# GpSimd's first root moved between its scatters, and its fifth scatter put behind the next group's first scores

## The reference

```python
x = x + conv_ref(_ln_c(x), W_qkv, b_qkv, W_proj, b_proj)   # windowed attention
t = _to_tokens(x)
t = t + ffn_ref(_ln_t(t), router_w, w1, w2, w3)            # mixture of experts
...
def _ln_c(v, eps=1e-06):
    m = jnp.mean(v, axis=-1, keepdims=True)
    s = jnp.var(v, axis=-1, keepdims=True)
    return (v - m) / jnp.sqrt(s + eps)
```

## Time and profile before

| what | us |
|---|---|
| median of 3 runs | 703.29 |
| range of the runs | 696.98 to 704.82 |
| the profiled execution's own time | 693.54 |
| its span, first to last instruction | 691.2 |
| PE busy | 593.7 (86%) |
| DVE busy | 484.2 (70%) |
| GpSimd busy | 440.0 (64%) |
| ACT busy | 414.2 (60%) |

### The profile page before, as it was taken

How to read it: one execution, slowest core, us unless ns; L and a number is a source line. 1 busy time by engine, 2 the same in 40 slices (tenths; PEclk the granted TensorE clock), 3 DMA queues, 4 the chain that set the end, 5 groups by cost and what they waited for, 6 DMA issues and landing times.

```text
span 691.2 us, 20144 instructions
## 1 busy us (share of the span) xinstructions
PE 593.7 (86%) x5359; PEld 368.5 (53%) x5359; DVE 484.2 (70%) x1692; ACT 414.2 (60%) x934; POOL 440.0 (64%) x398
## 2 busy tenths in 40 slices
PE   1888888888888888852889999999999999999991
PEld 0466566656665556542445555555555555555550
DVE  2578878888878767763556667777676777776772
ACT  1678777778767767641345556555565565565560
POOL 1111777767767766546557876775766868666776
PEclk9999999999999999965599999999999999999996
DMA  9900000100000000001143444444434434344342
GB/s 328 295 10 9 26 27 25 33 25 25 25 24 25 24 23 24 26 25 37 45 85 39 53 43 44 50 41 48 50 38 50 44 43 52 38 50 48 38 52 16
DMA packets 85590, 34.67 MB, mean 50 GB/s; under 512 B 81966, under 2 KB 82478, under 8 KB 85038
## 3 DMA queue, kind: packets, MB, share of 16 engines
q0 software_dynamic: 26640, 9.90, 15.0%
q1 hardware_dynamic: 58910, 24.30, 14.3%
HBM read 20.21 MB, written 13.76 MB: 49 GB/s over the span
## 4 chain that ended last, share of the span: by engine, by line
PE 51%; issue 7%; DMA 5%; POOL 5%; DVE 4%; POOLq 1%; ACT 1%; DVEq 0%; ACTq 0%
PE bank L504 21%; PE bank L518 13%; POOL expert_rows L1225 3%; PE bank L473 3%; DMA expert_rows<-rows,slot_u 3%; PE bank L451 2%; PE bank L509 2%; PE bank L441 2%; PE bank L463 2%; PE bank L634 2%; DMA out<-y_early,meta 1%; PE bank L528 1%; DMA out<-y_out,token 1%; DVE smax L960 1%; PE bank L435 1%
## 5 line engine op out<-in xcount | busy, mean ns | idle before, releaser
L1313 POOL DMA_INDIRECT out<-y_out,token x144 | 222.8, 1547 | 89.2 <-DVE y_out L1136 53.1
L1225 POOL DMA_INDIRECT expert_rows<-rows,slot_u x144 | 147.8, 1027 | 79.2 <-issue 27.5
L504 PE MATMUL bank<-xs,w_sb 64*128 64x384 f32 x510 | 182.2, 500 | 4.7 <-DVE hid L1175 1.8
L505 PE MATMUL bank<-xs,w_sb 64*128 64x384 f32 x510 | 182.5, 501 | 0.0
L779 ACT ACTIVATE gate_h<-bank 128x384 f32<-128x384 f32 x255 | 125.2, 492 | 61.2 <-PE bank L505 43.6
L1175 DVE TENSOR_TENSOR hid<-gate_h,bank 128x384 f32<-128x384 f32 x255 | 140.4, 554 | 30.2 <-ACT gate_h L779 13.2
L504 PEld LDWEIGHTS bank<-xs,w_sb 64*128 64x128 f32 x510 | 92.0, 189 | 88.2 <-issue 39.4
L518 PE MATMUL bank<-hid,w_sb 128*64 128x384 f32 x612 | 110.5, 496 | 2.7 <-DVE hid L1175 2.7
L505 PEld LDWEIGHTS bank<-xs,w_sb 64*128 64x128 f32 x510 | 92.0, 189 | 0.0
L789 ACT ACTIVATE y_odd<-bank 64x384 f32<-64x384 f32 x51 | 24.9, 487 | 85.9 <-PE bank L518 82.0
L1168 DVE TENSOR_TENSOR y_t<-y_odd,bank 64x384 f32<-64x384 f32 x51 | 27.8, 546 | 56.3 <-ACT y_odd L789 53.4
(11 more groups left out here) (136 smaller groups left out, 977.2 us busy)
## 6 DMA issues: line engine op xcount, KB each, us to landing
xin<-expert_rows SPq DMA_DIRECT2D x51, 99.0 KB
xin<-expert_rows SPq DMA_DIRECT2D x51, 96.0 KB
w_sb<-w SPq DMA_DIRECT2D x1, 3072.0 KB, 22.1
out<-res_all SPq DMA_DIRECT2D x18, 128.0 KB
expert_rows<-rows,slot_u POOLq DMA_INDIRECT x144
out<-y_out,token POOLq DMA_INDIRECT x144
x_all<-x_win SPq DMA_DIRECT2D x1, 1664.0 KB, 8.6
res_all<-x_res SPq DMA_DIRECT2D x1, 1664.0 KB, 12.1
```

Source lines behind the costliest of these rows:

```text
L504: pe.matmul(ps_h[c % RING], w13_sb[0:C, e, c, :], xs[0:C, :], start=True, stop=True)
L505: pe.matmul(ps_g[c % RING], w13_sb[C:2 * C, e, c, :], xs[C:2 * C, :], start=True, stop=True).then_inc(s_h, 1)
L1225: pool.indirect_dma_start(rows_dram, bass.IndirectOffsetOnAxis(ap=slot_u[:, spar, i // 2, i % 2:i % 2 + 1], axis=0), rows[:, spar, i // 2, ...
L1313: pool.indirect_dma_start(out, bass.IndirectOffsetOnAxis(ap=token[:, c:c + 1], axis=0), y_out[:, c, :], None, compute_op=ALU.add).then_inc ...
```

## The change

Only GpSimd's program is edited. Root 1 comes directly behind scatter 1. Scatters 2 and 3 follow it back to back, and the wait in front of scatter 2 is gone. The wait in front of scatter 4 is a new one: `scored(b)` waits until PE has finished the first scores of the next group (`s_score` reaches b + 1, which is the first score instruction of the next pass) instead of until DVE has subtracted in the fourth tile of this group.

```diff
+            def scored(tg):
+
+                after(pool, s_score, tg, 0)
+                hold(pool)
+
...
                 elif ok(send):
                     fill_meta(send, par)
                     scatter(par, (0, 1), par)
-                    softened(att_g, 2)
-                    scatter(par, (2,), par)
                 if ok(new):
                     root(ln1_rstd, ln1_vare, s1vare, s1rstd, s1xn, new)
                 if ok(send) and not drain:
-                    scatter(par, (3,), par)
-                    softened(att_g, 3)
+                    scatter(par, (2, 3), par)
+                    scored(b)
                     scatter(par, (4, 5), par)
```

## The result

In alternating runs on one chip the changed kernel took 704.45 us (median of 20 runs, 700.37 to 708.11) and the kernel before 700.0 us (20 runs, 695.93 to 705.45). The ratio is 1.0049, with a 95% interval of 1.0027 to 1.007: the change costs 1.9 to 4.9 us, and the forecast was a gain of 1.6. The time lies inside the range; the sign is wrong.

A forecast was written before the change was run, and what follows sets the result against it. The prediction took a circle of waits between DVE and PE as the bound, GpSimd outside it but disturbing L830. Terms of -1.4 and -0.2 us made -1.6, from 703.29 to 701.7 us, range 695.5 to 707.

The forecast's parts named there:

- The gain of 1.4 us from L830: DVE's L830, no longer beside scatter 2, takes 0.17 us less in 8 passes where PE waits for q: 1.4 us.
- 0.17 us less, with the q rotation behind it: In DVE's list, L830 falls from 0.34 us by 0.17 us, and q starts that much sooner.
- the 0.2 us: DVE's L858 takes 0.17 us, 0.03 less in 8 unmasked passes, before the next softmax: 0.2 us gained.
- covers: Slack before readers need GpSimd's later results; thinnest at L821 behind the centring, 0.77 us against 0.45 late in unmasked passes.
- the late centring: Rival, chance 0.09: DVE's L821 waits for GpSimd's centring in every pass; net 4.4 us slower, 707.7 us.
- Nothing comes of it: Rival, chance 0.12: PE's gap before L634 is largely its own issue, so earlier q buys little: 703.3 us.
- The disturbance only moves: Rival, chance 0.10: scatter 4 starts sooner and holds L858 as L830 was; 1.1 us come back, 703.0 us.
- L858 sits out scatter 4: Rival, chance 0.08: DVE's L858 is held until scatter 4 ends, 0.47 us more in 8 unmasked passes: 705.7 us.
- Within 1%: Whole kernel's time within about 1% (7 us) of the kernel before, chance 0.83; faster 0.09, slower 0.08.
- the spread of the runs: Rival, chance 0.15, on the whole time: three runs of one kernel lie 7.8 us apart, against terms of 1.6 us.

The follow-up runs named there:

- centring first: The changed kernel with the centring placed ahead of scatter 6, against the kernel before: 0.9998 on chip 4, 1.0118 on chip 10.
- the new wait alone: The kernel before with only scatter 4's wait changed to the next group's first scores, root 1 unmoved: 0.9969 on chip 2, 0.9988 on chip 3.
- PE by pairs: PE's loop unrolled to two passes per turn; on chip 4 the change so edited took 684.8 us, the kernel before so edited 1.0002 against 684.25 us unedited.
- those that lost 7%: Root 1 moved but scatter 4's old wait kept (1.0706 to 1.078), the same with PE's loop unrolled (1.0768), and the change without any wait before scatter 4 (1.0778).
- the last two kernels: The kernel before with, between scatters 3 and 4, a second scatter 3 (1.0065) or a GpSimd product without a DMA (1.0124), on chip 14.

## Why the prediction was wrong

**The gain of 1.4 us from L830 was none.** L830 does take 0.16 us in every pass, as foretold, but q starts no sooner. In the row of the pass above, L834 starts 0.19 us and q (L970) 0.53 us behind L830's start. In the kernel before, at 88.97, q starts at 89.50: the same 0.53 us, with L830 at 0.34. Over the passes to 275 us it is 0.52 or 0.53 in all 12 of before, the one with the short L830 among them, and in all 11 of the change. These are L834 and q of before in the pass of the earlier trace rows:

```profile
89.16 0.42 DVE L834 TENSOR_REDUCE ln_sum<-res_all 128x4 f32 x1
...
89.50 0.74 DVE L970 SCALAR_TENSOR_TENSOR q_st<-bank,wqkv_sb,consts 128x512 f32<-128x512 f32 x1
```

L834 starts at 89.16, while L830's row runs until 89.31. The longer row lengthened the end of L830, not DVE's line. It is no sign either that scatter 2 kept DVE from a port: L834 starts while that scatter still runs (to 89.35). The step "0.17 us less, with the q rotation behind it" failed, and the trace of before held the answer: the next start on the engine counts, not the length of the row. The same holds of L858 (0.17 instead of 0.20, and L890 starts 0.13 or 0.14 us behind its start in both), so that the 0.2 us were none either. On chip 4, where PE's signals are not late, nothing is gained either: the change with the centring first stands at 0.9998 [0.9982, 1.0014].

**Root 1** starts 0.14 us behind L830's end and moves nothing, as forecast. **Scatters 2 and 3** are plain, 1.03 and 0.96 us, as forecast.

**Scatter 4** is 0.96 us instead of 1.38, as forecast, but starts 5.28 us behind L830's end (129.37 - 124.09) instead of 4.3. The forecast took the end of PE's row as the moment of release; the release came 0.74 us behind that row, 0.81 behind scatter 3. On chip 4 it started 4.48 us behind L830's end by the same wait (124.99 - 120.51), near the forecast.

**Nobody waits for scatters 4 and 5: this is the step that failed and costs the time.** I listed who waits for GpSimd's list (root 2, centring, scatter 7, the small copies, the drain), and each of these covers held: L821 never waited, so the late centring, my rival on the slow side, did not come. What I did not list is that a signal of PE given while a scatter runs can come late, and who waits for PE then. This is a term that the sum put at nothing without a reason.

Counted from L830's start, scatter 5 ends at 6.44 us before (94.45 + 0.96 - 88.97) and at 7.66 now (131.59 - 123.93), 1.22 us later. L1006 starts at 7.14 before (96.11), where DVE comes just then and does not wait, and at 8.40 now, 1.26 us later, after 1.18 us idle. The seven unmasked passes are then 0.9 to 1.6 us longer each than the same pass of before. With the new wait alone scatter 5 ends at 6.9 us and L1006 starts at 7.6, between the two. The old order's wait ahead of scatter 4 held scatters 4 and 5 where their end plus 0.7 us fell on DVE's arrival; the change used up that room. On chip 4 L1006 does not wait for L463 in any pass from 80 to 275 us, with the new order or the old.

**The rivals.** "Nothing comes of it" is right of the gain, for another reason than PE's own issue. "The disturbance only moves" needed scatter 4 close behind scatter 3, which did not happen. That L858 sits out scatter 4 was not met by the change (L858 ends at 129.04, scatter 4 starts at 129.37), but it was with the new wait alone, on chip 3:

```profile
110.01 0.96 POOL L1225 DMA_INDIRECT expert_rows<-rows,slot_u  x1 [1.90 <-PE bank L441]
110.30 0.17 DVE L858 TENSOR_SCALAR ln_vare<-ln_var 128x4 f32<-128x4 f32 x1
```

L858 starts 0.29 us into the scatter and takes 0.17: it does not sit it out, and that rival falls.

**The chances.** Within 1% had 0.83 and came true in the result. That the time lies inside the range is owed to the width that was given for the spread of the runs, not to the mechanism. On chip 10 the change lost 1.06% (the interval reaches from 0.26 to 1.87), and on chip 4 its two variants, PE by pairs and centring first, lost nothing; so a spread between chips, which three runs of one kernel could not show, belonged beside the spread between runs.

**What stays open.** Shown is where and when PE and its signals are late, that the delay follows the scatters in time, and that it is on chips 2, 3 and 10 and not on 4; on chip 14 neither of the two kernels profiled shows it, but none of those that lost 7% ran there. What in the chip does it is not: whether it is the scatters' descriptors, their packets or GpSimd being busy was to be told by the last two kernels, and they met a chip without it. Nor is it shown whether the single matmuls and the late signals are one effect or two. Nor is it shown why a row of four costs so much more than two rows of two. Holding back SyncE's store of the residual, which starts in the same place, was not tried.

## What to carry to other kernels

Before a shorter row is counted as a gain, look at the start of the next instruction on its engine, with the long and with the short row: if the distance between the starts is the same, the gain is nothing. When scatters are moved, ask also who takes signals of PE while they run, not only who waits for GpSimd's list; a wait in a row of scatters was worth some 7% on three chips here, and taking it out must be tested by itself. And repeat a small effect on a second and third chip before explaining it: two edits here seemed to remove the loss because they ran on a chip that does not have it.

## What the hardware showed that I had not expected

- On three of five chips, PE's signals that are given while scatters run can reach their readers late: L1006 started 0.6 to 0.8 us behind the end of scatter 5 in the changed kernel, and the copy L727 up to 2.5 us behind the end of PE's own row where the scatters had been moved beside it. The distance to the scatter's end is not the same everywhere: in two later passes of the kernel before L1006 starts 0.34 and 0.36 us behind the end of scatter 6. On chip 4 the scores released scatter 4 within 0.05 us of their row's end, with the usual 0.78 us to its start taken off, and L1006 started 0.10 us behind PE's row in the middle of scatter 5.
- There, under an unbroken row of four scatters, PE starts one matmul about every 0.73 us until 0.76 to 0.85 us behind the row's end, in L463 as in L451.
- The kernel before itself takes 684 us on chips 4 and 14 and 694 to 701 on the other three. By two profiles the difference is not in the seven unmasked passes (108.8 us in the one shown, 108.9 with PE by pairs on chip 4) but in the five behind them (85.4 against 77.9 us). In the one shown L1006 waits in all five of these, 5.2 us in all, and on chip 4 in none. In the first of the five, ACT's L693 has waited 1.24 us when it starts at 189.01, 1.13 us behind the end of L451's row, with scatter 5 beside it until 188.63; on chip 4 it starts there without a wait. So the kernel before seems to pay for late signals too, and an order that puts its scatters elsewhere in those passes may gain there; that was not tried.
- A row of DVE can be twice as long beside a scatter (0.34 against 0.16 us) and the engine's next starts be the same to 0.01 us (L834 and L970 in 23 passes).
